# Unread products ahead of six normalisation steps, and a new order of steps, in a one-core transformer block

## The reference

```python
x = x + attn(cond(x, cond_1024[:, None, :], ...), ...)
x = x + ffn(cond2(x, cond_1024, weight), Wg, bg, Wi, Wo, A, B)
# cond: logmap0, layer_norm, modulation by rows made from cond_1024 (norm),
#   q, k, v with norms per head (qkv, heads), softmax attention with 16 heads (att),
#   output product (outp), mobius_add (fin), second norm and modulation (norm2),
#   two products of the feed-forward without a nonlinearity between (ff), mobius_add (fin2)
# attn: projections (proj), local attention in windows of 64 and attention to
#   64 pooled latents (maxi for the maxima, loc for the rest), gates and w_out (mix)
# ffn: router with top 2 of 4 experts, base product + low-rank term, relu, Wo (moe)
```

## Time and profile before

| what | value |
|---|---|
| median of 3 runs | 1186.57 us (1186.52 to 1190.21) |
| the profiled execution | 1185.35 us, its span 1183.5 us |
| TensorE busy | 1120.4 us, 95% of the span |
| VectorE, ScalarE, GpSimd busy | 863.6, 677.8, 240.9 us (73, 57, 20%) |
| mean granted clock of TensorE | 0.991 of full |
| chain that ended last | PE 74%, ACT 9%, DVE 9%, issue 4%, POOL 3% |

### The profile page before, as it was taken

How to read it: one execution, slowest core, us unless ns; L and a number is a source line. 1 busy time by engine, 2 the same in 40 slices (tenths; PEclk the granted TensorE clock), 3 DMA queues, 4 the chain that set the end, 5 groups by cost and what they waited for, 6 DMA issues and landing times.

```text
span 1183.5 us, 32775 instructions
## 1 busy us (share of the span) xinstructions
PE 1120.4 (95%) x13168; PEld 804.7 (68%) x13168; DVE 863.6 (73%) x3425; ACT 677.8 (57%) x1415; POOL 240.9 (20%) x336
## 2 busy tenths in 40 slices
PE   6878979999999999999999999999999999998998
PEld 3545545676677677777777677777777777776776
DVE  6898968978878887869676885877477895653333
ACT  1677757567755756575665746557474744443231
POOL 2222022042112230221203220122203220210111
PEclk9989979999999999999999999999999999999999
DMA  9510100001000001010000101000001000000000
GB/s 332 147 48 15 37 16 16 25 26 45 25 16 29 28 3 55 2 42 29 29 15 5 44 2 34 15 21 15 11 12 34 15 17 19 3 20 20 3 19 19
DMA packets 27353, 38.59 MB, mean 33 GB/s; under 512 B 3536, under 2 KB 21328, under 8 KB 27200
## 3 DMA queue, kind: packets, MB, share of 16 engines
q1 hardware_dynamic: 25296, 34.29, 9.0%
q10 hardware_dynamic: 1904, 2.20, 0.6%
HBM read 31.79 MB, written 4.29 MB: 30 GB/s over the span
## 4 chain that ended last, share of the span: by engine, by line
PE 74%; ACT 9%; DVE 9%; issue 4%; POOL 3%; DMA 1%; ACTq 0%; DVEq 0%; POOLq 0%
PE psg L455 45%; PE psq L455 17%; PE pso L455 7%; PE psg L458 6%; ACT PQ L1450 3%; POOL M L1797 2%; ACT M L1450 1%; DVE nm L992 1%; DMA QK<-in_w 1%; ACT JA L1461 1%; DVE JD L1005 1%; DVE R L989 1%; ACT QK L1450 1%; POOL R L1822 1%; DVE sf L989 0%
## 5 line engine op out<-in xcount | busy, mean ns | idle before, releaser
L1450 ACT ACTIVATE PQ<-psq 128x2048 f32<-128x2048 f32 x112 | 210.2, 1876 | 66.2 <-PE psq L455 65.7
L1822 POOL TENSOR_TENSOR R<-R,rhoT 128x256 f32<-128x256 f32 x128 | 92.7, 746 | 424.3 <-ACT R L1450 424.3
L455 PE MATMUL psq<-QK 32*128 32x128 f32 (+5 forms) x3360 | 128.1, 302 | 1.8 <-DMA QK<-in_w 1.8
L455 PE MATMUL psg<-zT,WiT 128*128 128x256 f32 x480 | 114.5, 381 | 2.1 <-DVE R L989 1.9
L455 PEld LDWEIGHTS psq<-QK 32*128 32x128 f32 (+2 forms) x3360 | 97.0, 165 | 25.7 <-issue 18.3
L455 PE MATMUL pso<-PQ,Vg 128*32 128x256 f32 (+2 forms) x2048 | 109.4, 345 | 4.5 <-ACT PQ L1450 2.4
L455 PE MATMUL psg<-WoT,R 128*128 128x256 f32 x480 | 107.9, 380 | 0.0
L992 DVE TENSOR_REDUCE nm<-psq 128x16 f32<-128x2048 f32 (+1 forms) x48 | 92.8, 1933 | 20.5 <-PE psq L455 19.8
L1450 ACT ACTIVATE R<-psg 128x512 f32<-128x512 f32 x60 | 35.7, 595 | 113.5 <-PE psg L455 113.2
L455 PEld LDWEIGHTS psg<-WoT,R 128*128 128x128 f32 x480 | 89.3, 190 | 13.1 <-issue 1.2
L455 PEld LDWEIGHTS psg<-zT,WiT 128*128 128x128 f32 x480 | 86.9, 190 | 15.4 <-DVE R L989 2.6
(11 more groups left out here) (236 smaller groups left out, 2272.8 us busy)
## 6 DMA issues: line engine op xcount, KB each, us to landing
bcB<-ada_rows SPq DMA_DIRECT2D x16, 384.0 KB, 3.4
bcA<-ada_rows SPq DMA_DIRECT2D x15, 384.0 KB, 3.3
X<-in_x SPq DMA_DIRECT2D x16, 256.0 KB, 3.0
XR<-in_x SPq DMA_DIRECT2D x16, 256.0 KB, 2.7
out<-XR SPq DMA_DIRECT2D x15, 256.0 KB, 2.1
QK<-NMT SPq DMA_DIRECT2D x96, 4.0 KB
WiT<-in_WiT SPq DMA_DIRECT2D x1, 1024.0 KB, 5.1
WoT<-in_WoT SPq DMA_DIRECT2D x1, 1024.0 KB, 7.7
```

Of the source, the lines that this page charges most:

```text
L455: return e.matmul(o, lhsT, rhs, start=start, stop=stop, skip_group_check=True)
L1450: return e.activation(o, i, func, **kw)
L1822: e.tensor_tensor(R4, R4, rhoT[:, :], ALU.mult).then_inc(*pool_moe.mark(b, f"r{f}{j}"))
```

## The change

Two things are changed. `idle(bank, n)` issues n products of the bfloat16 identity with itself, repeated four times to 512 columns, into a bank that nobody reads before the transposes overwrite it. It is called with n = 5 in `norm(b)` for b from 1 to 4 and in `norm2(b)` for b 0 and 1, when the bank is taken and before the wait for GpSimd. And all five strings of `ORDER` are other permutations of the same steps; the first 63 letters of TensorE are the same.

```diff
 ORDER = {
     "PE": [
-        "A*An*qqqq******hh*a**aa*aaanaaooqqqqnoohhqqaqqaaanaaahaqhooaqqaqaaoaaoaNahooFFhanaaqoaaoaaqqaqoopppppphh",
+        "A*An*qqqq******hh*a**aa*aaanaaooqqqqnoohhqqaqqaaanaaahaqhooaqqaaqaoaaoNaahoohFFanaaqaoaqoaaqaqopoppppphh",
...
+            def idle(bank, n):
+
+                for _ in range(n):
+                    mm(bank.rearrange("p (k n) -> p k n", k=4), identb[:, :], identb[:, :].unsqueeze(1).broadcast_to([128, 4, 128]),
+                       True, True)
+
...
                 bank = take(pg, ("mT", b), act_norm.at(b, "mT"))
                 if not b:
                     w.wait_ge(*pool_setup.at(0, "identb"))
+                if 1 <= b < 5:
+                    idle(bank, 5)
                 w.wait_ge(*pool_norm.at(b, "m1"))
                 turn4(bank, M1).then_inc(*pe_norm.mark(b, "T"))
...
                 bank = take(pg, ("mT2", b), act_norm2.at(b, "mT"))
+                if b < 2:
+                    idle(bank, 5)
                 w.wait_ge(*pool_norm2.at(b, "m1"))
                 turn4(bank, M2).then_inc(*pe_norm2.mark(b, "T"))
```

More of the change, by code:

```diff
@@ new lines @@
+        "ffofFfoFfoFfnFfnFfnFfnFfnFfnFfnFfoFfoFfoFoFoFoooooqggfgfgfgfgfgfgqgggggqgogogggggggggqgfgfqfofofofqpfqfo",
+        "fqfofqfqfsfqfofqfoqfoqfofqfohhhhpfopfofsososooomffffffPmPPPoPoPPPmPfmPfPfPfPfPfPfPfPfPfPfPfPfPPfPfPfPfPf",
+        "PfPfPfPfPfPfPPPPPPPfPfPfPfffNNNNNnNnNnnnnnFFFFFFFoFoFoFoFFoFqFoFooooogogoqoogogoggqqgwgwgwgwgwgwNgwNgwNg",
+        "wNgwNgNgNoogggqgfwqgqgqfqnqnqnfqfnqfnqfnqfnhhhhefgefgefefefefeeFefefefefFefFepeFeFfeFfeFfeFfeFfeFfeFqeFs",
+        "FsFfFfsfsfffPPPPPPPPepPgpPgPPPPgPgPgPgPgPgPgPgPgePgPgPgPgPgPgPgPgPgmePqPgPgmePqPgPgPPPPgmPgPmeeqNNNNqNNN",
@@ new lines @@
+        "qqFqqqFqFqFqFnqFnqFnhFnFnFnFnFFFFhhhpogogosossosoooooooogogogogoggggNgNgNgNNNNggqggggggggggowowgwwfwfFfF",
+        "wfFwfFwfFfFfFfwfFwfqfFfFFfFfFfFfqpfFpffffffqfgmwfqfmfqfqfpqngqngqmqngqngqngmqngqnghgsgsgsgsgggggggggggge",
+        "eeeghhhegeeeoeoeoeoeeeeeooeoeoeoeoeoqoeqoeooooqqwwoowwwwwfwfqffffqfqfqfqfwfqwfqfqfqfqfqphpffffffffwffmff",
+        "fpfmPePsmPePssmPsPePPPPPPPPPPePPPPPPPPPPPPPPPPPPPPPPPPPPPeeNNNNNNNnnhhhnnnnnFFoFoFoFoFoFFFoFoFoFoFoFqFoo",
+        "oooggoogggggggggggeeegegegqgegqwgNwgNogNogNegNegNewNewewewgwegweffFwfewfFfefFfefFfefFepfFpfFewfFefFefFef",
@@ new lines @@
+        "FfFfFfFfFffffffffgfgfqggmegggggmeggqggmqeqnqmqeqngqngqngqngqngqnghhhhogoggggggeeooooopooooosossosoooooww",
+        "ffffwfwfwfwfwfwffffeeeefefefefefqfefwfewfqfefeeeeeqfpfpfefefefePePePePwPPPPPPPPPPPPmPPPPPPqPPmPePmPePPPm",
+        "PPqPePqPqPqPqPqPqPqPqPqPqheNNNNNnNnNnnnnneehhhFFoFoFoFoFoFFFoFoFoFoFoFoFqopogogososogsgsggggggggggggggoo",
+        "NgNgNgNgNgNfNfgfffffgwfwfgfwfewfewfefefefFfefefefFwfFwfFwfFefFeFewFewfqfFefFefFefqfFeFewFeFpepegegeqeggg",
+        "mqggqmqeqnmqeqngqmqnqeqngqnghngngeggggggggggggggeehhhpoosossosoooooooooooooooffqfffffffffffffwfwffefefwf",
@@ new lines @@
+        "ewfewfewfewewefefwfwfeqfefePePeqpPepPePePePePePePePePPPPPPPPPPwPPPPPmPpPqPPPPPPPPmPePPPPPPmemNeNNNNNNFFe",
+        "FFFFFFFFFFFFFgggggggggggeeggggggogogogooNgNgNgNgNNNoooooooqoooooqnqnqnqnqnqnqnqqqhhhhgoogfqqfffffqqqwfwf",
+        "wfwfqwqwqwfqwqwqwqfnqfnqfnqfnhfpfnpfnfnfffffwffmfeFfefefmeFepemeFeFemeFeFeFeFeFeFeFeFeFeFeFeeeggeggggggg",
+        "ghhheogoggegggogoogoeogogogogogogoooogogeeoofffffffqfffqfffqfffffffwfwffefewewewfwfwefwfewfwfeqePePePePe",
+        "PePePePePePpepePewePePePPPPPPPPPPPPPPPPPPPPPPPPPmePPqPPmqemqeqPqmqqqqqqhNNneNnNnNnNnNnneehhhFFoFoFoFoFoF",
@@ L94 @@
[L94 removed]
+        "nnnn****nnnnnnnnffnnnnNNNNffnnnnggffffnnNNNNnnggNNNNfnnnnfeeggeeeeeeNNNNnnnnggNNNNffggnnnnffeeeeeeeennNN",
+        "NNnnggNNNNffggeeeeeennnneeffeeeeeeeenNNNNnnnggNNNNffggnnnneeeeeeeeffeeeeNNNNeeeeggNNNNnnnnffnnnnggeeeeee",
+        "eeffeeeeeeennNNNNnneggNNNNffeeeeeeeeffggeeeeeeeeNNNNggNNNNffeeeeeeggeeNNNNggeeeeeeeeeeeeeeeeeeeeeeeeeeee",
         "eeeeeeeeeeee",
```

82 lines of the change are left out of this document (30 added, 52 removed).

## The result

The changed kernel takes 1191.99 us (median of six, 1191.06 to 1194.35), the kernel before 1187.17 us in the same session (six, 1186.52 to 1190.21). The ratio is 1.0040 with a 95% interval of 1.0028 to 1.0052, 4.8 us. I had said 1185.5 us, 1180 to 1191: the time lies above the range, and slower was the side to which I had given 0.23.

What follows compares the result with a forecast made beforehand. TensorE was taken to bound the kernel from 200 to 1040 us, with early waits before. Products +3.5, waits removed -5.1, waits added +4.1, clock -3.6 gave -1.1 us: 1185.5 us from the 1186.57 us median, range 1180 to 1191 us.

Steps and rivals of the forecast that it cites:

- What bounds the kernel: Before 200 us TensorE waits for others; from 200 to 1040 us it is the bound, so added work there adds time.
- The unread products: Five products at six norm places, 1.15 us per place, partly hidden in waits: +3.5 us in all.
- What the order takes away, -5.1 us: Early TensorE waits filled: maxima -1.4, ST ahead of feed-forward -1.2, local attention -2.0, h0T copy -0.5 us.
- The wait for h0T, -0.5 us: Batch 0's wait of 0.79 us for the h0T copy gets four transposes to cover it: -0.5 us.
- The +1.1 us at batch 4: Batch 4's last values step follows the one before at once and waits for its exponential: +1.1 us.
- The -1.4 us at the maxima: At batch 0's maxima OS's transposes shorten a 2.42 us wait to 1.8, and wo's 0.78 us wait goes: -1.4 us.
- The local attention, -2.0 us: In the first local attention, transposes and a QKV product cover the wait of 2.04 us at 192.18 us: -2.0 us.
- the chain of batch 0, +3.0 us: Batch 0's mixing to its router: close-set steps wait for copies 1.1, norm 6 0.8, short mixing steps 1.1 us: +3.0 us.
- Past 215 us, 0 with 2.5 on either side: Behind 215 us the same work is shuffled with few waits: 0, give or take 2.5 us.
- The clock, -3.6 us: Of three half-clock stretches (about 62-68, 152-156, 162-166 us), worth 5.4 us, two of three were taken as gone: -3.6 us.
- early chain becomes the bound: Rival: late M for norm 6 or bcB rows for batch 2's second norm stall TensorE: 1190.3 us, chance 0.15.
- the products don't do what they are there for: Rival: low-clock stretches remain or others come while 3.5 us are paid: 1189.1 to 1191 us, chance 0.08 beyond the bound.

Runs made afterwards that it cites:

- e1: The changed kernel without its unread products, so the new order alone: 1192.61 us, ratio 1.0038.
- s3: The kernel before with the new order only behind TensorE's step 432 (about 450 us), no unread products: 1191.36 us, ratio 1.0028.
- l1: The kernel before with batch 0's second local scores moved ahead of norm 6's transposes, and ScalarE's exponentials to match: 1191.29 us, ratio 1.0020.
- e3: The kernel before with OS's transposes moved between batch 0's first and second maximum, VectorE's steps to match: 1187.69 us, ratio 1.0004.
- s2: The kernel before with the new order only in the middle piece, TensorE's steps 116 to 432, no unread products: 1188.72 us, ratio 1.0005.
- e2: The kernel before, in its own order, with the five unread products at the same six places: 1190.13 us, ratio 1.0018.
- p1: The kernel before, in its own order, with ten unread products instead of five at each of the six places: 1196.02 us, ratio 1.0064.
- t1: The new order up to TensorE's step 432, the order of before behind it, no unread products: 1189.36 us, ratio 1.0011.
- e4: The changed kernel with two feed-forward products of batch 2 moved between batch 0's z products and its router's products: 1195.72 us, ratio 1.0065.
- s1: The kernel before with the new order only up to TensorE's step 116 (about 172 us), no unread products: 1193.13 us, ratio 1.0040.

## Why the prediction was wrong, step by step

- **What bounds the kernel**: held. Up to 200 us TensorE waits for others, and after that idle time is time: from 240 to 1040 us 2.2 us more of it cost 3.3 us.
- **The unread products**: right in mechanism in the old order, a little high in size. Predicted 1.15 us for five, measured 1.09; predicted +3.5 us in all, measured +3.0 in the old order and +2.2 in the new one up to step 432. The Trainium skill (TensorE: Matmul & The Clock Gate, Wait — 56ns, not 53.3ns?) gives 215.7 ns for one of 512 columns; ten of them took 54.03 - 51.86 = 2.17 us here, 217 ns each, so the trace agrees. Norm 2 hid them as said (2.58 us of wait left, "near 2.5"). The second norm of batch 0, which I gave 1.15 us, hid most of them too: of the 1.02 us for OT and 0.42 us for O that the order alone has at 112 to 114 us, after has 0.22 and 0.30 us left.
- **What the order takes away, -5.1 us**: a step that failed, the first in time. I took each wait as a reserve of its own. The waits of TensorE up to the end of batch 4's attention show it, before, from 60 to 175 us:

```profile
PE psq L455 <- ACT PQ L1450: 8.0, 6, 2.2
...
PE psq L455 <- DVE nm L992: 2.4, 1, 2.4
...
PE pso L455 <- ACT OT L1453: 0.6, 1, 0.6
```

And in the run with the order alone, which is some 3 us behind by then, from 60 to 178 us:

```profile
PE psq L455 <- ACT PQ L1456: 7.0, 6, 2.0
...
PE psq L455 <- DVE nm L998: 3.1, 2, 1.8
PE pso L455 <- ACT OT L1459: 1.9, 2, 1.3
...
PE pso L455 <- ACT PQ L1456: 0.7, 1, 0.7
...
PE psg L458 <- DVE hy L989: 0.5, 1, 0.5
```

The wait of 1.20 us for ST went, and PQ ahead of score steps fell from 8.0 to 7.0 us. But nm rose from 2.4 to 3.1 us, OT ahead of values steps from 0.6 to 1.9, and new are 0.7 us for PQ there and 0.5 us for hy. All rows of this view together are 22.3 us before and 23.7 us in e1; three more profiles with the order of before or one exchange there (s3, l1, e3) have 21.9 to 22.9 us up to 176 us. So a predicted -2.0 us (-1.4 - 1.2 - 0.5 + 1.1) came out above 0. Of its terms the -1.2 us came as said. The wait for h0T, -0.5 us, stayed (0.79 us before, 0.7 in e1). The +1.1 us at batch 4 was near: 2.25 us of wait before, 1.01 + 1.29 + 0.69 = 2.99 us in e1, and 1.00 us at the last values step in s2. The -1.4 us at the maxima is the term that was wrong. At the maxima the three waits were 2.42 + 0.78 + 1.45 = 4.65 us before; the order alone has 1.83 + 1.25 + 1.63 = 4.71 us, at 151.77, 156.52 and 159.56 us. The first shrank to 1.8 us and the one before wo went, as predicted, and one of 1.25 us for VectorE came ahead of the third maximum. My working priced TensorE's gap and not VectorE's queue, in which the maxima follow one another.
- **The local attention, -2.0 us, and the chain of batch 0, +3.0 us**: the first as said, the second 4.1 us in the run with the order alone, 1.1 more than I had. The middle piece should then cost 2.1 us, and it cost 1.8. Norm 6, put at 0.8 us, waited 0.50; the router's products waited 0.93 us, as worked out from ScalarE's pair of copies.
- **Past 215 us, 0 with 2.5 on either side**: the largest miss. Behind step 432 alone (about 450 us) it is +3.3 to +3.9 us, beyond the bound that I had set. I reasoned that the same work with few waits stays so, and priced no step of the new order there. What the runs show in its place are new waits for maxima, for a zT copy and for R. My reading is that a stretch with 11 us of idle time in 800 has little to win from another order and something to lose wherever one engine hands over to another.
- **The clock, -3.6 us**: failed in size, and in the step from one stretch to the total. No low stretch went in the profiled run, and over its runs the changed kernel had a mean clock of 0.9913, where before had 0.9888 to 0.9897 in the later sessions: about 1.5 to 2.4 us given back. The second stretch did answer to the order, as I had said: in the profiles of the six kernels with the old order at the maxima (before, e2, s2, s3, l1, p1) wo ran there in 3.72 to 3.75 us, and of the eight with OS's transposes moved seven had it in 1.99 us; after, with 3.13 us, is the exception. But all fourteen have a low stretch at the place of the first and one at that of the third, which I had also left to the order, and others came: up to 240 us TensorE stood at the low level (by windows of 1 us) for 20.5 to 27.3 us in the six and 17.1 to 30.7 us in the eight, 23.9 us in the mean of either. I read three stretches of one execution as fixed properties of the program, and priced the one that went as if nothing took its place.
- **The sum**: 1.4 (order to step 432) + 3.6 (behind it) + 2.2 (products) - 1.5 (clock) = +5.7 us, for 4.8 us measured. Mine was -1.0 (-5.1 + 4.1) + 0 + 3.5 - 3.6 = -1.1 us. The order is 6.0 of the 6.8 us between the two sums, the clock 2.1, and the products take 1.3 back. The clock's -1.5 us rests on six runs of after and is its least certain term.

The rival "early chain becomes the bound", 1190.3 us, was near in time and wrong in mechanism: neither norm 6 nor bcB's chain decided. The rival "the products don't do what they are there for", 1189.1 to 1191 us, was right that low stretches remain or others come, and wrong about the size: its 4.1 us of new waits against 5.1 us of gains were my own terms, and those failed. What stays open is how the 1.1 to 2.0 us of the last piece that its idle time doesn't show come about (3.3 less 2.2 us in s3, 3.9 less 1.9 us between t1 and e1), and whether the products do raise the clock in the new order.

## What to carry to other kernels

A wait in a trace is worth what is left of it once the next late engine is asked for: before an order is changed to fill it, read on each other engine when the step behind it could be ready, and price the gap only down to that. Where an engine is busy 98% of a stretch, another permutation of the same work can win little and cost more, here 3.3 to 3.9 us; keep the old order there and change only the part that waits. Before a clock stretch is counted as gain, look at several executions of the same code.

## What the runs showed of the hardware

- Runs of the same kernel differ by up to 9 us (before, 25 runs of one session: 1184.74 to 1193.53), and most of that follows the mean granted clock, from 0.984 to 0.993, at 0.95 us for 0.001. The Trainium skill (TensorE: Matmul & The Clock Gate, Part 1: The HAM clock gate) calls the number of slow matmuls at a kernel's start run-variable; the runs agree that it varies (7 of 14 profiles have a low stretch at 14 to 22 us, four of the eight with SyncE's order of before and three of the six with its new one), and not at the start alone.
- Waits of the same length fell on either side. Behind a wait of 2.04 us in the first local attention before ran on at the full clock, while in e3, with the same steps and the same wait of 2.04 us at 192.93 us, the clock was 0.66 from 193 to 198 us. A wait of 2.79 us (e4) and one of 3.62 us (s1) had low clock behind them.
- Filling a wait at one place moved the clock at that place, and not the mean. With the wait of 2.42 us shortened wo ran at the full clock in seven of eight profiles, and yet the mean clock of the exchange alone was 0.9885 over eleven runs; and filling six places with products that only keep TensorE busy left it at 0.9901 and, with twice as many, 0.9892.
- The largest loss of clock, 0.9851 over eight runs, went with one new early wait of 3.62 us, but part of the low time stood well behind it, at 200 to 202 us. The second largest, 0.9875 over eleven runs (l1), had no such wait: its longest new one is 1.85 us.
